# A two-layer decoder on one core: ScalarE takes over the scaled x and fifteen of sixteen final norm steps in the last feed-forward

## The chip, the cores and the metric

One core of a Trainium2 chip runs the whole program. The metric is the device time of one execution in microseconds; lower is better. The engines are TensorE (PE), VectorE (DVE), ScalarE (ACT), GpSimd (POOL) and SyncE (SP, which issues the DMAs). Each has its own instruction queue, works it off in order, and waits for the others by semaphores.

## The reference

Two decoder layers on x of 8 x 256 x 512, each with self-attention, cross-attention and a feed-forward; after each of the six a residual sum and a layer norm, (x - mean) / sqrt(var + 1e-5). The change touches the sixth alone, a feed-forward with 8-bit floats (e4m3) and one scale per tensor:

```python
def _fp8_matmul(x2d, w):
    scale_x = jnp.maximum(jnp.max(jnp.abs(x2d)) / 448.0, 1e-06)
    scale_w = jnp.maximum(jnp.max(jnp.abs(w)) / 448.0, 1e-06)
    x8 = (x2d / scale_x).astype(jnp.float8_e4m3fn)
    w8 = (w / scale_w).astype(jnp.float8_e4m3fn)
    return jnp.matmul(x8.astype(x2d.dtype), w8.astype(x2d.dtype).T) * (scale_x * scale_w)
h = _fp8_matmul(x2d, w_fc)           # 2048 x 512 by 512 x 2048
h = jnp.square(jax.nn.relu(h))
out = _fp8_matmul(h, w_proj)         # 2048 x 2048 by 2048 x 512
x = _layernorm(x + out, axis=-1)     # and this is the output
```

Since h is scaled by its own maximum, no part of the second product can start before all of the first is known.

## The kernel before

The six parts run one after the other; x (2048 rows of 512) stays in SBUF as sixteen tiles of 128 x 512 (`x_all`). The last part, `fp8_ffn_1` (L2096), has two blocks of code with a full stop of all engines between them.

**The first block** (L2135 to L2279) computes the first product into `kept`. x is taken in eight chunks c of two tiles (`x_of(c)`, 128 x 1024). Of each chunk ACT makes `raised` (L2198: the absolute value times a factor, bf16) and POOL makes `value` (L2279: x times the inverse scale, f32); DVE rounds to e4m3 from both, two operations in `round_e4m3` (L1123, L1125); PE turns the result (`turn`, L2159, 8 transposes); ACT copies it out of PSUM into `xT` (L2202). `raised`, `value` and `rounded` have two buffers each, so chunk c waits until chunk c-2 is rounded. Chunks 0 and 1 are done ahead. Then come NB = 4 batches n of 512 columns, each of NG = 8 groups k of 8 matmuls (L2169) into one of three pairs of PSUM banks; ACT evicts each group with Relu (L2215) and DVE takes its maximum (L2247). Within batch n the next two chunks are woven in: DVE rounds them behind k = 1 and 4, PE turns them behind k = 3 and 6, ACT copies them at k = 4 and 6 and makes `raised` of the two after these at k = 5 and 7 (for n = 0 and 1).

**The second block** (L2300 to L2385) handles the 32 groups of `kept` in order, u = 8 n + k. ACT squares a group twice (L2324, L2325), DVE rounds it in two operations (L2347, L2352), and PE multiplies (L2314, 8 matmuls). Rings of RING = 4 buffers join them: ACT may square group u once DVE has rounded group u - 4. A batch's sums lie in PSUM in four tiles t. They are finished while the next batch is rounded: `fin` (DVE: L2331 adds the residual, L164 and L166 take mean and variance), the inverse root on POOL (`root_of`: L174, L176), and `apply` (DVE L181: subtract the mean, multiply by the root, in place). In the batch after, `fin` of tile t stands behind DVE's group k by `FINS`, `apply` by `APPLIES` (L2105). For the last batch all four tiles are finished behind the last group. SP stores each pair of tiles once both are applied (L2382 to L2384).

Of the kernel before, what the change touches and what calls it, by code (L numbers as in the profile page):

```python
# [11 lines left out]
ALU = mybir.AluOpType  # L12
# [7 lines left out]
QT = S // P  # L20
# [2075 lines left out]
def fp8_ffn_1(nc, g, w8, out):  # L2096
# [7 lines left out]
    FINS = {1: 0, 2: 1, 4: 2, 5: 3}  # L2104
    APPLIES = {2: 0, 4: 1, 5: 2, 6: 3}  # L2105

    with ExitStack() as mem:
# [16 lines left out]
        topped, spread = g.sem("f1_top_ready"), g.sem("f1_top_spread")  # L2124
        valued, raised_s = g.sem("f1_x_scaled"), g.sem("f1_x_raised")
        xlinked, xrounded, turned, copied = (g.sem("f1_x_" + n) for n in ("link", "rounded", "turned", "copied"))
# [8 lines left out]
        with nc.Block() as block:  # L2135
# [55 lines left out]
            @block.scalar  # L2191
            def _(eng):
                def raise_x(c):
                    if c == 0:
                        eng.wait_ge(w8.linked, 6)
                    if c >= 2:
                        eng.wait_ge(xrounded, c - 1)
                    eng.activation(raised[c % 2], x_of(c), ACT.Abs, scale=w8.raise_by[:, 0:1]).then_inc(raised_s, 1)  # L2198

                def copy_x(c):  # L2200
                    eng.wait_ge(turned, c + 1)
                    eng.activation(xT[:, :, c * S:(c + 1) * S], g.R[:, 2 + c % 2, :].bitcast(BF16).rearrange("p (k n) -> p k n", k=KD),  # L2202
                                   ACT.Copy).then_inc(copied, 1)

                raise_x(0)
                raise_x(1)
                copy_x(0)
                copy_x(1)
                raise_x(2)
                raise_x(3)  # L2210
                for n in range(NB):
                    for k in range(NG):
                        use = n * NG + k
                        eng.wait_ge(up_full, use + 1)
                        eng.activation(kept[:, n, k, :], pairs[use % 3].rearrange("p j n -> p (j n)"), ACT.Relu).then_inc(up_kept, 1)  # L2215
                        if n < NB - 1 and k in (4, 6):
                            copy_x(2 * n + 2 + (k == 6))
                        if n < NB - 2 and k in (5, 7):
                            raise_x(2 * n + 4 + (k == 7))

            @block.vector
            def _(eng):
                def round_x(c):
                    eng.wait_ge(valued, c + 1)
                    eng.wait_ge(raised_s, c + 1)
                    if c >= 2:
# [44 lines left out]
            @block.gpsimd  # L2271
            def _(eng):
                eng.memset(ones[:, :], 1.0).then_inc(filled, 1)
                for c in range(B):
                    if c == 0:
                        eng.wait_ge(w8.linked, 6)
                    if c >= 2:
                        eng.wait_ge(xrounded, c - 1)
                    eng.tensor_scalar(value[c % 2], x_of(c), w8.inverse[:, 0:1], None, ALU.mult).then_inc(valued, 1)  # L2279

# [6 lines left out]
        downed, summed, stats = g.sem("f1_down_added"), g.sem("f1_sum_ready"), g.sem("f1_stats_link")  # L2287
        applied_v, stored = g.sem("f1_norm_by_vector"), g.sem("out_stored")

# [10 lines left out]
        with nc.Block() as block:  # L2300
# [17 lines left out]
            @block.scalar  # L2318
            def _(eng):
                for u in range(NB * NG):  # L2320
                    group = kept[:, u // NG, u % NG, :]
                    if u >= RING:
                        wait_rounded(eng, u - RING)
                    eng.activation(raised[u % RING], group, ACT.Square, scale=raise_root)  # L2324
                    eng.activation(group, group, ACT.Square, scale=root).then_inc(squared, 1)  # L2325

            @block.vector
            def _(eng):
                def fin(n, t):
# [4 lines left out]
                    if n:  # L2334
                        eng.wait_ge(applied_v, TILES * (n - 1) + t + 1)
                    norm_statistics(eng, stats, TILES * n + t, x_tile(n, t), st[t]).then_inc(gathered, 1)

                def apply(n, t):
                    eng.wait_ge(rooted, before["root"] + TILES * n + t + 1)
                    norm_apply(eng, x_tile(n, t), x_tile(n, t), st[t]).then_inc(applied_v, 1)  # L2340

                links = 0
                for u in range(NB * NG):
# [9 lines left out]
                    if n and k in FINS:  # L2353
                        fin(n - 1, FINS[k])
                    if n and k in APPLIES:
                        apply(n - 1, APPLIES[k])
                for t in range(TILES):
                    fin(NB - 1, t)
                    if t:
                        apply(NB - 1, t - 1)  # L2360
                apply(NB - 1, TILES - 1)

            @block.gpsimd
            def _(eng):
                def root_of(n, t):
                    done = TILES * n + t
                    eng.wait_ge(gathered, before["stats"] + done + 1)  # L2367
                    norm_root(eng, rooting, before["rooting"] + POOL_ROOT_STEPS * done, st[t], 1e-5, g.minus_half[:, :]).then_inc(rooted, 1)
                    eng.wait_ge(rooted, before["root"] + done + 1)

# [9 lines left out]
            def _(eng):  # L2380
                for b in range(B):
                    eng.wait_ge(applied_v, QT * (b + 1))  # L2382
                    dst = out.rearrange("b (t p) d -> p b t d", p=P)[:, b:b + 1]
# [99 lines left out]
```

## Time and profile before

| | |
|---|---|
| median of 3 runs | 2383.47 us (2379.13 to 2386.53) |
| the profiled execution, its own time | 2388.34 us |
| its span, first to last instruction | 2386.4 us |
| first block, from ones L2273 to the last maximum | 2175.1 to 2261.3 us |
| second block, first square to last apply | 2266.8 to 2383.2 us |
| busy share of the whole span: PE, DVE, ACT, POOL | 86%, 68%, 50%, 33% |
| mean granted TensorE clock (share of full speed) | 0.945 |

All times in rows count from the start of the span. The last feed-forward is the last 211 us of it. A row of a timeline gives the start, the duration in us, the engine, the line, what is written <- what is read with their shapes, how many such instructions it merges (x4), and in brackets how long the engine had been idle before and who ended that. Two ACT or DVE instructions in a row overlap a little: the next starts about 0.1 us before the one in front has ended, so steps of the work are read from start to start.

### The profile page before, as it was taken

What the parts mean: (1) busy time and instruction counts of PE and PEld (TensorE: products, weight loads), DVE (VectorE), ACT (ScalarE), POOL (GpSimd) and SP (SyncE); (2) the same over time, 40 slices, a digit from 0 to 9 for tenths busy, and PEclk for the clock granted to TensorE, in tenths of its full rate; (3) what the DMA queues carried; (4) which work ended last, traced back from release to release, by engine and by line L of the source; (5) the groups of instructions that cost most, each with busy time, mean ns of one, the idle gap of its engine ahead of it and who ended that gap; (6) DMA issues with size and microseconds to landing.
All of it is one profiled execution on the core that took longest, in us unless ns stands there. A gap on an engine that the chain in (4) does not pass through costs nothing. (4 is left out here: it accounts for less than half of the span.)

```text
span 2386.4 us, 39689 instructions
## 1 busy us (share of the span) xinstructions
PE 2049.2 (86%) x14893; PEld 1744.1 (73%) x14900; DVE 1627.6 (68%) x3672; ACT 1203.7 (50%) x3119; POOL 780.5 (33%) x817
## 2 busy tenths in 40 slices
PE   6999999379999988799978789999999999984764
PEld 5899988267777777577758678888888988883321
DVE  3677777547767675688865645567676776765798
ACT  3666555256666665334333334445555554343583
POOL 1223222476666664344431111111111112223112
PEclk8999999689999998899989889999999999997998
DMA  4111121200000000521110031224233322100101
GB/s 163 55 54 54 41 72 63 80 5 6 5 5 6 5 1 1 194 98 36 37 37 12 1 141 63 86 93 163 89 111 133 111 80 85 60 21 36 36 18 53
DMA packets 51781, 143.87 MB, mean 60 GB/s; under 512 B 4604, under 2 KB 15869, under 8 KB 46728
## 3 DMA queue, kind: packets, MB, share of 16 engines
q1 hardware_dynamic: 51592, 141.34, 16.6%
q8 instruction: 120, 1.97, 0.3%
q14 instruction: 69, 0.57, 0.1%
HBM read 111.95 MB, written 29.36 MB: 59 GB/s over the span
## 5 line engine op out<-in xcount | busy, mean ns | idle before, releaser
L2032 POOL TENSOR_TENSOR x_probs<-x_probs,x_total 128x512 f32<-128x512 f32 x128 | 133.4, 1042 | 588.3 <-DVE x_total L2002 588.1
L1953 ACT ACTIVATE x_probs<-x_probs,x_nmax 128x256 f32<-128x256 f32 x256 | 128.3, 502 | 259.4 <-DVE x_nmax L1992 259.4
L140 DVE TENSOR_TENSOR x_probsT_lo<-banks,x_probsT_hi 128x512 fp32r<-128x512 f32 x256 | 168.0, 682 | 52.5 <-ACT x_probsT_hi L134 52.1
L134 ACT ACTIVATE x_probsT_hi<-banks 128x512 fp32r<-128x512 f32 x256 | 145.1, 604 | 105.9 <-PE banks L1887 83.3
L597 PE MATMUL banks<-x_turned,x_wq_hi 128*128 128x256 f32 x1024 | 185.8, 283 | 9.8 <-DVE x_turned L140 9.8
L597 PE MATMUL banks<-x_probsT_hi,x_V_hi 128*128 128x256 f32 x512 | 152.0, 297 | 33.5 <-DVE x_probsT_lo L140 33.5
L597 PEld LDWEIGHTS banks<-x_turned,x_wq_hi 128*128 128x128 f32 x1024 | 157.3, 189 | 11.1 <-DVE x_turned L140 11.0
L902 POOL TENSOR_TENSOR x_probs<-x_probs,x_total 128x960 f32<-128x960 f32 (+1 forms) x128 | 131.8, 1051 | 93.8 <-DVE x_total L1054 93.8
L589 POOL TENSOR_TENSOR a_probs<-a_probs,a_total 128x512 f32<-128x512 f32 (+1 forms) x64 | 95.0, 1494 | 174.6 <-DVE a_total L559 174.6
L1011 ACT ACTIVATE x_probs<-banks,x_nmax 128x240 f32<-128x240 f32 x256 | 115.1, 471 | 67.2 <-DVE x_nmax L1042 67.2
L597 PE MATMUL banks<-x_probsT_lo,x_V_hi 128*128 128x256 f32 x512 | 147.5, 288 | 0.0
L597 PE MATMUL banks<-x_probsT_hi,x_V_lo 128*128 128x256 f32 x512 | 147.5, 288 | 0.0
L597 PE MATMUL banks<-x_turned,x_wq_lo 128*128 128x256 f32 x512 | 143.7, 281 | 0.0
L1309 POOL TENSOR_TENSOR f_hid_lo<-f_hid,f_hid_hi 128x256 fp32r<-128x256 f32 x128 | 94.1, 735 | 141.6 <-ACT f_hid_hi L134 141.2
L597 PEld LDWEIGHTS banks<-x_probsT_hi,x_V_hi 128*128 128x128 f32 x512 | 100.5, 196 | 43.1 <-DVE x_probsT_lo L140 41.1
L1290 ACT ACTIVATE f_act<-f_z 128x256 f32<-128x256 f32 x128 | 53.4, 417 | 151.0 <-DVE f_z L1361 150.8
L523 ACT ACTIVATE a_probs<-banks,a_nmax 128x128 f32<-128x128 f32 (+1 forms) x256 | 104.4, 425 | 39.8 <-DVE a_nmax L549 39.3
L1272 PE MATMUL banks<-f_downT,f_hid_hi 128*128 128x512 f32 x256 | 111.0, 434 | 1.6 <-POOL f_hid_lo L1309 1.6
L597 PE MATMUL banks<-x_wo_hi,x_oT_hi 128*128 128x512 f32 x256 | 105.0, 410 | 2.6 <-DVE x_oT_lo L140 2.6
L2314 PE MATMUL banks<-f_weights,f_xT 128*128 128x512 bf16 x256 | 67.2, 413 | 44.2 <-DVE f_xT L2352 44.2
L597 PEld LDWEIGHTS banks<-x_probsT_lo,x_V_hi 128*128 128x128 f32 x512 | 100.7, 197 | 0.9
L597 PE MATMUL banks<-x_wo_lo,x_oT_hi 128*128 128x512 f32 x256 | 101.0, 395 | 0.0
(452 smaller groups left out, 7075.9 us busy)
## 6 DMA issues: line engine op xcount, KB each, us to landing
x_turned<-x_parked SPq DMA_DIRECT2D x24, 1536.0 KB, 6.5
x_parked<-x_turned SPq DMA_DIRECT2D x8, 1536.0 KB, 5.8
x_raw_q<-in_L_xattn_Wq_dram SPq DMA_DIRECT2D x5, 1024.0 KB, 5.2
x_raw_o<-in_L_xattn_Wo_dram SPq DMA_DIRECT2D x5, 1024.0 KB, 8.2
x_all<-in_x_dram SPq DMA_DIRECT2D x2, 2048.0 KB, 18.0
a_sign_raw<-in_L_ffn_W_g_dram SPq DMA_DIRECT2D x8, 512.0 KB, 3.9
f_parked<-a_sign_turned SPq DMA_DIRECT2D x16, 256.0 KB, 2.4
a_sign_raw<-in_L_ffn_W_u_dram SPq DMA_DIRECT2D x8, 512.0 KB, 3.7
```

Source lines behind the costliest of these rows:

```text
L134: return eng.activation(out, in_, ACT.Copy, scale=scale)
L140: return eng.tensor_tensor(out, in_, high.bitcast(F32), ALU.subtract)
L523: ins = eng.activation(probs[u % NP][:, r, 0:keys], banks[:, r, :], ACT.Exp, bias=nmax[:, u, r:r + 1], accum_out=total[:, u, r:r + 1])
L589: eng.tensor_tensor(probs[u % NP][:, :, 0:keys], probs[u % NP][:, :, 0:keys], total[:, u, :].unsqueeze(2).to_broadcast([P, G4, keys]), ALU ...
L597: ins = eng.matmul(out, lhs, rhs, start=start and n == 0, stop=stop and n == len(steps) - 1)
L902: ins = eng.tensor_tensor(tile, tile, total[:, u, n, :].unsqueeze(2).to_broadcast([P, G4, c1 - c0]), ALU.mult)
L1011: eng.activation(probs[u % NP][:, r, 0:MAIN], g.S[:, r, 0:MAIN], ACT.Exp, bias=nmax[:, u, r:r + 1], accum_out=total[:, u, 0, r:r + 1])
L1272: ins = eng.matmul(g.S[:, 2 * b.parity + t, :], h[:, t * P:(t + 1) * P], downT[:, m, :], start=m == 0 and n == 0, stop=m == HT - 1 and n == 1)
L1309: eng.tensor_tensor(hid_lo[buf][:, :], hid[buf][:, :], hid_hi[buf][:, :].bitcast(F32), ALU.subtract).then_inc(low, 1)
L1953: ins = eng.activation(probs[t][r][:, j, :], probs[t][r][:, j, :], ACT.Exp, bias=nmax[:, t, r, j:j + 1], accum_out=total[:, t, r, j:j + 1])
L2032: eng.tensor_tensor(probs[t][r][:, :, :], probs[t][r][:, :, :], total[:, t, r, :].unsqueeze(2).to_broadcast([P, 2, S]), ALU.mult).then_inc ...
L2314: ins = eng.matmul(accumulator(n, t), hidden[u % RING][:, at:at + P], proj[h][:, :, m + j, :], start=k == 0 and j == 0, stop=k == NG - 1 a ...
```

## The change

- `value` of each chunk is made by ACT (`activation` Copy with a scale pointer) just ahead of `raised`, and POOL's L2279 is gone with its semaphore. In the opening, ACT's order is now scale 0, scale 1, copy 0, scale 2, copy 1, scale 3.
- `apply` of fifteen tiles is made by ACT: Identity(x * root + offset), where the offset, -mean * root, is a new 128 x 1 operation on POOL behind L176. In batch n ACT applies tiles 0, 1, 2 of batch n-1 behind its squares k = 5, 6, 7, and tile 3 of batch n-2 behind k = 0. Behind the last square it applies tile 3 of batch 2 and tiles 0 to 2 of batch 3. DVE keeps the last tile's apply.
- `fin` of DVE now waits for ACT's apply of the same tile number one batch back, as `st[t]` is used again; SP's stores wait for ACT's applies, the last one for DVE's too.

```diff
-    APPLIES = {2: 0, 4: 1, 5: 2, 6: 3}
+    APPLIES = {5: 0, 6: 1, 7: 2}
...
-                def raise_x(c):
+                def scale_x(c):
                     if c == 0:
                         eng.wait_ge(w8.linked, 6)
                     if c >= 2:
                         eng.wait_ge(xrounded, c - 1)
-                    eng.activation(raised[c % 2], x_of(c), ACT.Abs, scale=w8.raise_by[:, 0:1]).then_inc(raised_s, 1)
+                    eng.activation(value[c % 2], x_of(c), ACT.Copy, scale=w8.inverse[:, 0:1])
+                    eng.activation(raised[c % 2], x_of(c), ACT.Abs, scale=w8.raise_by[:, 0:1]).then_inc(valued, 1)
...
-                raise_x(0)
-                raise_x(1)
+                scale_x(0)
+                scale_x(1)
                 copy_x(0)
+                scale_x(2)
                 copy_x(1)
-                raise_x(2)
-                raise_x(3)
+                scale_x(3)
...
                         if n < NB - 2 and k in (5, 7):
-                            raise_x(2 * n + 4 + (k == 7))
+                            scale_x(2 * n + 4 + (k == 7))
...
                 eng.memset(ones[:, :], 1.0).then_inc(filled, 1)
-                for c in range(B):
-                    if c == 0:
-                        eng.wait_ge(w8.linked, 6)
-                    if c >= 2:
-                        eng.wait_ge(xrounded, c - 1)
-                    eng.tensor_scalar(value[c % 2], x_of(c), w8.inverse[:, 0:1], None, ALU.mult).then_inc(valued, 1)
...
             @block.scalar
             def _(eng):
+                def apply(n, t):
+                    eng.wait_ge(offset, TILES * n + t + 1)
+                    eng.activation(x_tile(n, t), x_tile(n, t), ACT.Identity, scale=st[t][:, 9:10], bias=st[t][:, 10:11]).then_inc(applied_s, 1)
+
                 for u in range(NB * NG):
...
                     eng.activation(group, group, ACT.Square, scale=root).then_inc(squared, 1)
+                    if n and k in APPLIES:
+                        apply(n - 1, APPLIES[k])
+                    if n > 1 and k == 0:
+                        apply(n - 2, TILES - 1)
+                apply(NB - 2, TILES - 1)
+                for t in range(TILES - 1):
+                    apply(NB - 1, t)
...
                     if n:
-                        eng.wait_ge(applied_v, TILES * (n - 1) + t + 1)
+                        eng.wait_ge(applied_s, TILES * (n - 1) + t + 1)
...
                     if n and k in FINS:
                         fin(n - 1, FINS[k])
-                    if n and k in APPLIES:
-                        apply(n - 1, APPLIES[k])
                 for t in range(TILES):
                     fin(NB - 1, t)
-                    if t:
-                        apply(NB - 1, t - 1)
-                apply(NB - 1, TILES - 1)
+                eng.wait_ge(rooted, before["root"] + TILES * NB)
+                norm_apply(eng, x_tile(NB - 1, TILES - 1), x_tile(NB - 1, TILES - 1), st[TILES - 1]).then_inc(applied_v, 1)
...
-                    eng.wait_ge(rooted, before["root"] + done + 1)
+                    if done < TILES * NB - 1:
+                        eng.wait_ge(rooted, before["root"] + done + 1)
+                        eng.tensor_scalar(st[t][:, 10:11], st[t][:, 6:7], st[t][:, 9:10], -1.0, ALU.mult, ALU.mult).then_inc(offset, 1)
...
                 for b in range(B):
-                    eng.wait_ge(applied_v, QT * (b + 1))
+                    eng.wait_ge(applied_s, min(QT * (b + 1), QT * B - 1))
+                    if b == B - 1:
+                        eng.wait_ge(applied_v, 1)
```

## Rows read from the trace of the kernel before

**Rows 1.** By stretch, busy us (x count) of PE, PEld, DVE, ACT, POOL; clock, DMA share, GB/s

```profile
2190.00:2260.00 70.00, 60.04 (x297) 27.51 (x302) 50.86 (x43) 43.77 (x44) 12.46 (x5) 0.98 0.05 15
2266.00:2374.00 108.00, 67.11 (x256) 24.36 (x256) 99.47 (x114) 68.59 (x64) 23.66 (x24) 0.89 0.08 30
```

**Rows 2.** Timeline of the first block's opening, all engines

```profile
2177.52 2.19 ACT L2198 ACTIVATE f_kept<-x_all,f_raise_by 128x1024 bf16<-128x1024 f32 x2 [15.05 <-DVE f_raise_by L1118]
2177.60 13.48 POOL L2279 TENSOR_SCALAR f_kept<-x_all,f_inverse 128x1024 f32<-128x1024 f32 x4 [2.25 <-DVE f_raise_by L1118]
2180.50 1.23 DVE L1123 SCALAR_TENSOR_TENSOR f_kept<-f_kept 128x1024 f32<-128x1024 bf16 x1 [3.01 <-POOL f_kept L2279]
2181.76 1.94 DVE L1125 SCALAR_TENSOR_TENSOR f_kept<-f_kept 128x1024 bf16<-128x1024 bf16 x1
...
2187.66 1.03 PE L2159 MATMUL banks<-ident,f_kept 128*128 128x128 bf16 x8 [2.87 <-DVE f_kept L1125]
2188.73 1.02 ACT L2202 ACTIVATE f_xT<-banks 128x1024 bf16<-128x1024 bf16 x1 [2.87 <-PE banks L2159]
...
2190.21 8.38 PE L2169 MATMUL banks<-f_xT,f_weights 128*128 128x512 bf16 x31 [1.52 <-ACT f_xT L2202]
```

**Rows 3.** Timelines of ACT, DVE and PE where batch 0 passes into batch 1

```profile
2210.46 1.14 ACT L2198 ACTIVATE f_kept<-x_all,f_raise_by 128x1024 bf16<-128x1024 f32 x1
2211.50 1.01 ACT L2215 ACTIVATE f_kept<-banks 128x1024 f32<-128x1024 f32 x1
...
2212.55 1.22 DVE L2247 TENSOR_REDUCE f_hmax<-f_kept 128x1 f32<-128x1024 f32 x1 [0.73 <-ACT f_kept L2215]
...
2215.18 1.22 DVE L1123 SCALAR_TENSOR_TENSOR f_kept<-f_kept 128x1024 f32<-128x1024 bf16 x1
...
2217.80 0.61 PE L2159 MATMUL banks<-ident,f_kept 128*128 128x128 bf16 x8 [1.40 <-DVE f_kept L1125]
```

**Rows 4.** Groups of ACT by form, whole span: busy us, mean ns | idle before

```profile
L1939 ACT ACTIVATE x_q_value<-x_q_raw,f_inverse 128x512 f32<-128x512 f32 x32 | 23.0, 719 | 0.0
L985 ACT ACTIVATE x_temp<-banks,x_norms_q 128x512 f32<-128x512 f32 x16 | 12.3, 772 | 0.2 <-POOL x_kT_lo L896 0.2
```

**Rows 5.** Timeline of DVE around the first finished tiles of the second block

```profile
2288.41 1.22 DVE L2347 SCALAR_TENSOR_TENSOR f_kept<-f_xT,f_kept 128x1024 f32<-128x1024 bf16 x1
...
2290.88 1.22 DVE L2347 SCALAR_TENSOR_TENSOR f_kept<-f_xT,f_kept 128x1024 f32<-128x1024 bf16 x1
...
2293.34 0.74 DVE L2331 SCALAR_TENSOR_TENSOR x_all<-banks,f_scaled,x_all 128x512 f32<-128x512 f32 x1
...
2294.95 1.19 DVE L2347 SCALAR_TENSOR_TENSOR f_kept<-f_xT,f_kept 128x1024 f32<-128x1024 bf16 x1
...
2299.42 1.22 DVE L2347 SCALAR_TENSOR_TENSOR f_kept<-f_xT,f_kept 128x1024 f32<-128x1024 bf16 x1
```

**Rows 6.** Waits, 2266 to 2374 us: who <- whom: us, times, longest

```profile
DVE f_kept L2347 <- ACT f_kept L2325: 2.7, 1, 2.7
```

**Rows 7.** Timeline of POOL behind the tiles begun at 2293.34 and 2297.39

```profile
2295.12 1.10 POOL L174 TENSOR_SCALAR f_st<-f_st 128x1 f32<-128x1 f32 x1 [67.34 <-DVE f_st L166]
2296.31 1.59 POOL L176 TENSOR_TENSOR f_st<-f_st,minus_half 128x1 f32<-128x1 f32 x1
...
2299.25 0.34 POOL L174 TENSOR_SCALAR f_st<-f_st 128x1 f32<-128x1 f32 x1 [1.35 <-DVE f_st L166]
```

**Rows 8.** Timeline of the tail behind the last group, DVE

```profile
2374.11 0.75 DVE L2331 SCALAR_TENSOR_TENSOR x_all<-banks,f_scaled,x_all 128x512 f32<-128x512 f32 x1 [2.00 <-PE banks L2314]
...
2375.73 0.72 DVE L2331 SCALAR_TENSOR_TENSOR x_all<-banks,f_scaled,x_all 128x512 f32<-128x512 f32 x1
...
2377.74 0.74 DVE L2331 SCALAR_TENSOR_TENSOR x_all<-banks,f_scaled,x_all 128x512 f32<-128x512 f32 x1
...
2382.66 0.55 DVE L181 TENSOR_SCALAR x_all<-x_all,f_st 128x512 f32<-128x512 f32 x1 [0.77 <-POOL f_st L176]
```

**Rows 9.** Timeline of PE in the second block, at the second pair of finished tiles

```profile
2302.03 5.31 PE L2314 MATMUL banks<-f_weights,f_xT 128*128 128x512 bf16 x16 [2.60 <-DVE f_xT L2352]
```

More of the change, by code:

```diff
@@ L2124, in fp8_ffn_1 @@
         topped, spread = g.sem("f1_top_ready"), g.sem("f1_top_spread")
-        valued, raised_s = g.sem("f1_x_scaled"), g.sem("f1_x_raised")
+        valued = g.sem("f1_x_scaled")
         xlinked, xrounded, turned, copied = (g.sem("f1_x_" + n) for n in ("link", "rounded", "turned", "copied"))
@@ L2224, in round_x @@
                     eng.wait_ge(valued, c + 1)
-                    eng.wait_ge(raised_s, c + 1)
                     if c >= 2:
@@ L2287, in fp8_ffn_1 @@
         downed, summed, stats = g.sem("f1_down_added"), g.sem("f1_sum_ready"), g.sem("f1_stats_link")
-        applied_v, stored = g.sem("f1_norm_by_vector"), g.sem("out_stored")
+        offset, applied_s, applied_v = g.sem("f1_norm_offset_ready"), g.sem("f1_norm_by_scalar"), g.sem("f1_norm_by_vector")
+        stored = g.sem("out_stored")
         def wait_rounded(eng, u):
@@ L2319, in _ @@
             def _(eng):
+                def apply(n, t):
+                    eng.wait_ge(offset, TILES * n + t + 1)
+                    eng.activation(x_tile(n, t), x_tile(n, t), ACT.Identity, scale=st[t][:, 9:10], bias=st[t][:, 10:11]).then_inc(applied_s, 1)
                 for u in range(NB * NG):
-                    group = kept[:, u // NG, u % NG, :]
+                    n, k = divmod(u, NG)
+                    group = kept[:, n, k, :]
                     if u >= RING:
@@ L2334, in fin @@
                     if n:
-                        eng.wait_ge(applied_v, TILES * (n - 1) + t + 1)
+                        eng.wait_ge(applied_s, TILES * (n - 1) + t + 1)
                     norm_statistics(eng, stats, TILES * n + t, x_tile(n, t), st[t]).then_inc(gathered, 1)
-                def apply(n, t):
-                    eng.wait_ge(rooted, before["root"] + TILES * n + t + 1)
-                    norm_apply(eng, x_tile(n, t), x_tile(n, t), st[t]).then_inc(applied_v, 1)
                 links = 0
```

## The prediction

> **What bounds the kernel now.** I read the page first. DVE is busy 68% of the whole span and PE 86%, but the change touches only the last 211 us, so the average says little. Next I read the busy time by stretch. While the first product runs (2190 to 2260 us) PE is busy 60.04 of 70 us, DVE 50.86, ACT 43.77, POOL 12.46; while the second is made (2266 to 2374) DVE is busy 99.47 of 108 us and ACT 68.59 [rows 1]. So PE leads the first block and DVE the second, and the timelines must confirm it.
>
> In the second block, DVE waits for ACT once, 2.7 us before its first group, and never again [rows 6]. From start to start a plain group takes 2290.88 - 2288.41 = 2.47 us of DVE, one with a `fin` behind it 2294.95 - 2290.88 = 4.07, one with `fin` and `apply` 2299.42 - 2294.95 = 4.47 [rows 5]. Every DVE operation taken out of this stretch shortens the path, as long as ACT keeps ahead.
>
> In the first block, the opening is a chain: POOL's `value` (until 2180.5), DVE's rounding, PE's turn, ACT's copy, the first matmul at 2190.21 [rows 2]. Later PE runs on without a break except before each of the six turns of chunks 2 to 7: there it waits 1.40 us for DVE's L1125 [rows 3].
>
> **The change part by part.**
>
> *1. The opening.* Before, DVE starts L1123 at 2180.50 behind POOL; L1125 takes 1.94 us beside POOL's next operation, against 1.22 for L1123's kind [rows 2, 3]. ACT's two operations on 128x1024 take 2.19 us together, so 1.04 from start to start and 1.15 the last [rows 2]. I price `value` on ACT like that. Then ACT makes value 0 at 2177.52, raised 0 at 2178.56, done 2179.71; L1123 starts at 2179.75 and L1125 at 2181.0; with POOL gone I give it 1.23, so it ends at 2182.25. The second chunk: ACT is done at 2181.8, DVE starts L1123 at about 2182.15 and ends L1125 at 2184.65. PE's second turn takes 1.03 and ends at 2185.75. Now ACT's order matters: copy 0 can start at 2183.35 (first turn done), takes 0.92 to the next start (1.02 less the overlap of 0.1), then scale 2 takes 2 x 1.04 us, so copy 1 starts at 2186.35, not at 2185.8. Before it started at 2188.73 [rows 2]. **Gain 2.35 us.** If L1125 keeps its 1.94 us without POOL, two of them give back 1.4, but 0.6 of that is hidden behind scale 2: the gain is at least 1.5. Scale 3 ends at 2189.5, ahead of the first eviction, 3.4 us or more behind the first matmul (then at 2187.85).
>
> *2. `value` inside the first block.* Chunks 4 to 7 cost ACT 1.04 us more each, at k = 5 and 7 of batches 0 and 1. At k = 5: the eviction of k = 6 slides by 1.04; PE has three pairs of banks and doesn't need it; the copy behind it slides by about 0.3 and is still done 0.4 before PE's batch ends. Cost nothing; the cover is the third pair of banks. At k = 7: before, ACT starts L2198 at 2210.46 and the next eviction (k = 0 of batch 1) at 2211.50, so the latter comes at 2212.54, 1.04 late; DVE's maximum L2247, before at 2212.55 directly behind it, comes at 2213.6, and with 1.14 us for each of two maxima from start to start, L1123 starts at 2215.9 where it was 2215.18. So rounding is 0.7 us later, and PE, which waited 1.40 us for it at 2217.80, waits 2.10 [rows 3]. This happens for batches 1 and 2. **Cost 2 x 0.7 = 1.4 us**, between 0 (a slack not seen) and the full 4 x 1.04 = 4.2. I take 1.4, since each step has its row.
>
> *3. Twelve applies leave DVE's loop.* Each costs 4.47 - 4.07 = 0.40 to 0.45 us there from start to start [rows 5]; I take 0.43. **Gain 12 x 0.43 = 5.2 us**, if ACT keeps ahead. ACT pays for them: an ACT operation of 128x512 from SBUF with a scale pointer takes 0.72 us, one from PSUM with scale and bias pointers 0.77 [rows 4]; I take 0.75. ACT has 108 - 68.6 us idle here [rows 1], so the amount is no problem; the order may be. An apply at the head of ACT's queue waits for POOL's offset, and the next group's squares are queued behind it, for which DVE waits, and PE behind DVE. The tightest place: `fin` of tile 3 starts on DVE at time F (k = 5). Its L166 is done about 1.7 us later; L174 starts at F + 1.8 and L176 ends at F + 4.56 (2295.12 and 2296.31 + 1.59 against 2293.34) [rows 5, 7]. The offset, a 128x1 operation like L174 but behind a DVE operation of 1.22 us, ends near F + 5.4. ACT, which has squared the group k = 0 long before, applies tile 3 until F + 6.15 and squares group k = 1 until F + 8.35 (2.2 us for the pair). DVE comes to this group at F + 1.61 + 3 x 2.47 = F + 9.0. Margin 0.65 us, at two places (k = 1 of batches 2 and 3); the other applies have more. POOL's chain is covered by the same margins.
>
> *4. The tail.* Four `fin` follow each other on DVE. Without an apply between them the step is 2375.73 - 2374.11 = 1.62 us, with one 2377.74 - 2375.73 = 2.01 [rows 8]; two of the three applies lie between (0.39 each), the third beside POOL's root. **Gain 0.8 us.** The last apply stays on DVE as it is; ACT's apply of tile 2 ends a good 1 us before it (offset 1.62 us ahead of the last tile's root, and 0.75 us on ACT). The last store starts with DVE's apply as before. The store ahead of it starts about 2.6 us before it instead of 3.3; each has 512 KB. Cost nothing, at most a few tenths.
>
> *5. New POOL operations.* Fifteen offsets, off the path except through the DVE. POOL's L174 took 1.10 us while DVE ran L2347, whose end at 2296.14 it survived by 0.08 us: POOL waits for DVE [rows 5, 7]. The other way: the DVE groups with POOL's L174 and L176 beside them are not longer than others (4.07 includes one) [rows 5]. Price 0; from above 12 x 0.35 us = 4.2, if each offset (L174 took 0.34 us when it started ahead of L2347 [rows 7]) holds DVE for its whole length.
>
> The Trainium skill, page "SBUF — State Buffer", section "SBUF: two separate sides", says that DVE and GpSimd share a port pair under an exclusive lock, taken for a whole instruction, and that whoever comes second is blocked entirely. For POOL the trace agrees (1.10 us, ending with L2347). For DVE it would make L1125 at 2181.76 wait for the POOL operation beside it; the row has 1.94 us, a slow-down and not a block. By the rule the sum would be that of rival A.
>
> **The sum.** 2.35 - 1.4 + 5.2 + 0.8 = 6.95, say 7.0 us less. The profiled execution would go from 2388.34 to 2381.3 (span 2386.4 to 2379.4). Against the median shown, 4.9 us lower than the profiled execution, it is 2383.47 - 7.0 = 2376.5 us, 0.29% less. What a measurement of this kernel can tell from no change is about 0.3% (7.2 us), so the forecast sits on that line.
>
> **The rivals.**
>
> *A. POOL's offsets hold DVE.* Twelve in the loop at 0.35 us: 4.2 us back, 2380.7. For: L1125's 1.94 us beside POOL. Against: POOL's 24 small operations in the second block show no such cost. Chance 0.10.
>
> *B. ACT falls behind in the second block.* If POOL gets through only when DVE has no two-operand work, the offset of tile 3 comes only when DVE stops for want of group k = 1 (F + 9.0). Then offset 0.35, apply 0.75, squares 2.2: DVE idle 3.3 us at two places, 6.6 us, 2383.1. For: L176 took 1.59 us. Against: it got through between L2352 and the next L2347. Chance 0.08.
>
> *C. ACT's added work in the first block reaches PE in full.* 4.2 us instead of 1.4, and 2379.3. For: ACT works without a pause from k = 4 to 7. Against: three bank pairs. Chance 0.11.
>
> *D. Slower than before: the clock falls in the first block.* PE waits 2.10 us instead of 1.40 before the turn in batches 1 and 2. In the second block PE is slow behind waits of that length: after 2.60 us, 16 matmuls take 5.31 us, 0.33 each [rows 9], where the first block's PE operations take 60.04 / 297 = 0.20 [rows 1]. A group of 8 is 1.6 us at 0.20 each, and at the lower of the two clock levels (1.2 GHz for 2.4) 1.6 us more. If each of the two longer waits leaves the clock low for the four groups to the batch's end, that is 8 x 1.6 = 12.8 us and 2389.3. It decides from the fifth such group (7.0 us are then gone). Against: PE is busy 60 of 70 us there and was granted 0.98 [rows 1], against 67 of 108 in the second block at 0.89. Chance 0.04.
>
> **How the numbers follow.** Forecast 0.67, A 0.10, B 0.08, C 0.11, D 0.04. The predicted time is the forecast's, 2376.5. Its own spread, from the bounds of the opening (1.5 to 2.35), the loop (0.40 to 0.45 each) and the three runs' scatter (2379 to 2387), is 2372.5 to 2380.5. The range reaches to A and C whole and most of B's side: 2371.5 to 2382. Faster by over 0.3% means below 2376.3: three fifths of the forecast, since what was not priced (matmuls closer together, hence a higher clock) is rather on this side: 0.40, and hardly anything else: 0.41. Slower by over 0.3% needs D or an unknown: 0.05. Within 0.3%: 0.54.
>
> **What would show it.** In the changed trace: the first matmul of L2169 10.35 us behind ACT's first L2198 or its successor, where it was 12.7 (2190.21 - 2177.52); L1125 at 1.23 us in the opening; PE waiting 2.1 us before the first turn of batches 1 and 2 and 1.4 before the others; second block from first square to last apply 110.4 us, where it was 116.45; DVE groups with `fin` at 4.07 and none at 4.47; DVE's L2347 waiting for ACT once only. Wrong it would be if L2347 waits for ACT at k = 1 of batches 2 and 3 (B), if L2347 or L2352 grow beyond 1.23 us (A), if PE waits for L2215 (C), or if matmuls between turns take 0.43 us (D).

## The result, and the profile after

| | before | after |
|---|---|---|
| median of 13 runs each | 2385.43 us (2379.13 to 2390.24) | 2379.01 us (2373.39 to 2384.40) |
| ratio, 95% interval | | 0.997 (0.9961 to 0.9979) |
| the profiled execution, its own time | 2388.34 us | 2379.84 us |
| its span | 2386.4 us | 2377.8 us |

0.3% less is 7.2 us of 2385; the medians themselves differ by 6.4. The predicted gain was 7.0. The predicted time, 2376.5 us, is 2.5 below the measured median and inside the stated 2371.5 to 2382; 2.0 of the 2.5 come from the median of before, which was 2383.47 over 3 runs and is 2385.43 over 13. Each kernel's runs spread over some 10 us, so the medians can't tell the steps apart. All ratios leave out two executions, of 2998 and 3938 us, that came up in the runs for the experiments. The stages of the two profiled executions can tell the steps apart:

| stage, from start to start | before | after | gain | predicted |
|---|---|---|---|---|
| span's start to ACT's first operation of this feed-forward | 2177.52 | 2175.82 | 1.70 | none: nothing is changed there |
| from there to the first weight load for L2169 | 12.28 | 9.88 | 2.40 | 2.35 |
| the weight load to the first turn inside the loop | 10.18 | 10.99 | -0.81 | 0 |
| ACT's first operation to the last maximum, the two rows above included | 82.53 | 82.25 | 0.28 | 0.95 |
| the last maximum to the first square | 6.70 | 6.70 | 0 | 0 |
| the first square to the end of the last apply | 116.46 | 109.82 | 6.64 | 6.0 |

The second and third rows share one point that has to be taken with care. The record of the first matmul of L2169 is missing in the trace of before (its row in [rows 2] has x31, and begins at 2190.21, while the weights were loaded from 2189.80 on), so I count from the weight load. The third row gives back 0.81 of the second row's 2.40: what counts is the fourth row. In these two executions the stages that the change touches gained 0.28 + 6.64 = 6.92 us; the other 1.70 us of the two spans' difference came before the changed code.

The traces of the experiments below show how much of this is the scatter of single executions. Up to the last maximum the first block takes 82.53 and 82.88 us in two traces with POOL's `value`, and 82.25, 82.39 and 82.59 in three with the change's opening and `value` on ACT: a gain of 0.28 is no larger than this spread. The second block takes 116.46, 117.27 and 117.20 us in three traces with DVE's applies, and 109.82 to 110.80 in seven with ACT's. That gain is plain in every pair.

The last maximum and the first square, before and then after (the last applies stand in [rows 8] and with the tail below):

```profile
2260.05 1.22 DVE L2247 TENSOR_REDUCE f_hmax<-f_kept 128x1 f32<-128x1024 f32 x1 [0.51 <-ACT f_kept L2215]
...
2266.75 1.15 ACT L2324 ACTIVATE f_xT<-f_kept,f_raise_by 128x1024 bf16<-128x1024 f32 x1 [6.73 <-PEq L2135]
```

```profile
2258.07 1.22 DVE L2247 TENSOR_REDUCE f_hmax<-f_kept 128x1 f32<-128x1024 f32 x1 [0.51 <-ACT f_kept L2216]
...
2264.77 1.15 ACT L2324 ACTIVATE f_xT<-f_kept,f_raise_by 128x1024 bf16<-128x1024 f32 x1 [6.73 <-PEq L2135]
```

The opening, as [rows 2] before. In this timeline the two products of ACT stand ahead of DVE's rounding:

```profile
2175.82 1.15 ACT L2198 ACTIVATE f_kept<-x_all,f_inverse 128x1024 f32<-128x1024 f32 x1 [15.03 <-DVE f_raise_by L1118]
2176.87 1.13 ACT L2199 ACTIVATE f_kept<-x_all,f_raise_by 128x1024 bf16<-128x1024 f32 x1
...
2178.03 1.22 DVE L1123 SCALAR_TENSOR_TENSOR f_kept<-f_kept 128x1024 f32<-128x1024 bf16 x1 [2.25 <-ACT f_kept L2199]
2179.29 1.23 DVE L1125 SCALAR_TENSOR_TENSOR f_kept<-f_kept 128x1024 bf16<-128x1024 bf16 x1
...
2184.64 1.01 ACT L2203 ACTIVATE f_xT<-banks 128x1024 bf16<-128x1024 bf16 x1
...
2185.70 0.13 PEld L2169 LDWEIGHTS banks<-f_xT,f_weights 128*128 128x128 bf16 x2 [1.97 <-ACT f_xT L2203]
2186.11 0.15 PEld L2169 LDWEIGHTS banks<-f_xT,f_weights 128*128 128x128 bf16 x1 [0.27 <-issue]
...
2190.38 0.15 PEld L2169 LDWEIGHTS banks<-f_xT,f_weights 128*128 128x128 bf16 x1 [0.28 <-issue]
2190.81 4.00 PEld L2169 LDWEIGHTS banks<-f_xT,f_weights 128*128 128x128 bf16 x19 [0.28 <-issue]
```

L1125 takes 1.23 us here, where it took 1.94 beside POOL [rows 2]. The weight loads then stand singly, 0.43 us apart, until 2190.81: eleven such rows. From there nineteen of them take 4.00 us together, 0.21 each. Before, there were seven single rows, until 2193.20. The stretches (columns as in [rows 1]) show what this is:

```profile
2185.70:2191.00 5.30, 5.29 (x13) 1.86 (x14) 0.61 (x1) 3.05 (x3) 0.00 (x0) 0.52 0.00 0
2191.00:2196.00 5.00, 4.30 (x20) 1.76 (x18) 3.64 (x4) 2.71 (x3) 0.00 (x0) 1.00 0.00 0
2188.30:2258.30 70.00, 58.98 (x299) 26.86 (x297) 51.08 (x44) 45.64 (x46) 0.00 (x0) 0.98 0.06 16
2264.00:2366.00 102.00, 68.22 (x255) 24.71 (x256) 93.97 (x102) 76.16 (x76) 38.37 (x36) 0.87 0.08 29
```

The sixth number is the granted clock, as a share of full speed. After the opening's waits PE was granted 0.52, its lower level, for 5.1 us, and then 1.00. Before, by the single rows, the lower level lasted 3.4 us. The last two rows answer to [rows 1]. PE still leads the first block, with POOL out of it. In the second, DVE has 93.97 us of 102 (92.1%; before 99.47 of 108, also 92.1%): it bounds that stretch as before, with twelve operations fewer.

Where batch 0 passes into batch 1, as [rows 3] before:

```profile
2208.21 1.14 ACT L2199 ACTIVATE f_kept<-x_all,f_raise_by 128x1024 bf16<-128x1024 f32 x1
2209.25 1.92 ACT L2216 ACTIVATE f_kept<-banks 128x1024 f32<-128x1024 f32 x2
...
2210.29 2.35 DVE L2247 TENSOR_REDUCE f_hmax<-f_kept 128x1 f32<-128x1024 f32 x2 [1.76 <-ACT f_kept L2216]
2212.55 1.22 DVE L1123 SCALAR_TENSOR_TENSOR f_kept<-f_kept 128x1024 f32<-128x1024 bf16 x1
...
2215.17 0.61 PE L2159 MATMUL banks<-ident,f_kept 128*128 128x128 bf16 x8 [2.05 <-DVE f_kept L1125]
...
2222.36 0.61 PE L2159 MATMUL banks<-ident,f_kept 128*128 128x128 bf16 x8 [1.40 <-DVE f_kept L1125]
```

The eviction starts behind two ACT operations, DVE's two maxima wait for it for 1.76 us (0.73 before), and PE waits 2.05 us before the turn. Before the six turns PE waits 1.39, 1.40, 2.05, 1.40, 2.06 and 1.40 us: two of six have grown by 0.65.

The second block, timelines of POOL, ACT and DVE, answering to [rows 5, 7]:

```profile
2288.89 1.22 DVE L2350 SCALAR_TENSOR_TENSOR f_kept<-f_xT,f_kept 128x1024 f32<-128x1024 bf16 x1
...
2292.96 1.19 DVE L2350 SCALAR_TENSOR_TENSOR f_kept<-f_xT,f_kept 128x1024 f32<-128x1024 bf16 x1
...
2297.01 1.19 DVE L2350 SCALAR_TENSOR_TENSOR f_kept<-f_xT,f_kept 128x1024 f32<-128x1024 bf16 x1
...
2305.95 0.75 DVE L2338 SCALAR_TENSOR_TENSOR x_all<-banks,f_scaled,x_all 128x512 f32<-128x512 f32 x1
...
2310.61 0.74 POOL L2371 TENSOR_SCALAR f_st<-f_st 128x1 f32<-128x1 f32 x1
...
2311.38 0.81 ACT L2317 ACTIVATE x_all<-x_all,f_st 128x512 f32<-128x512 f32 x1 [1.63 <-POOL f_st L2371]
2312.10 1.13 ACT L2324 ACTIVATE f_xT<-f_kept,f_raise_by 128x1024 bf16<-128x1024 f32 x1
2313.14 1.13 ACT L2325 ACTIVATE f_kept<-f_kept,f_scaled 128x1024 f32<-128x1024 f32 x1
...
2314.93 1.22 DVE L2350 SCALAR_TENSOR_TENSOR f_kept<-f_xT,f_kept 128x1024 f32<-128x1024 bf16 x1
```

A group with a `fin` takes 4.07 and 4.05 us of DVE, and none takes 4.47. The lower six lines are the narrowest place, group k = 1 of batch 2: the start of tile 3's `fin`, POOL's offset of this tile, ACT's apply (0.81 us, the next operation 0.72 behind its start), the two squares, ready at 2314.27 (2313.14 + 1.13), and DVE, which wants them at 2314.93: 0.66 us to spare. The waits of this stretch confirm it; DVE waits for ACT once, before its first group, as in [rows 6]:

```profile
DVE f_kept L2350 <- ACT f_kept L2325: 2.7, 1, 2.7
```

The tail, answering to [rows 8]:

```profile
2366.61 0.75 DVE L2338 SCALAR_TENSOR_TENSOR x_all<-banks,f_scaled,x_all 128x512 f32<-128x512 f32 x1 [2.00 <-PE banks L2309]
...
2368.23 0.72 DVE L2338 SCALAR_TENSOR_TENSOR x_all<-banks,f_scaled,x_all 128x512 f32<-128x512 f32 x1
...
2373.13 0.22 POOL L174 TENSOR_SCALAR f_st<-f_st 128x1 f32<-128x1 f32 x1 [0.34 <-DVE f_st L166]
...
2374.04 0.55 DVE L181 TENSOR_SCALAR x_all<-x_all,f_st 128x512 f32<-128x512 f32 x1 [0.99 <-POOL f_st L176]
```

From the first `fin` to the end of the last apply it takes 7.98 us (9.10 before): 1.12 us less. From there to the end of the span it is 3.2 us in both.

### The profile page after: what moved, and what is told of

Same layout as the page of the kernel before. It is cut to its first block and busy times, and to the rows that moved or that the text cites. A ratio compares the mean times of both kernels' runs of the same rounds, so it can differ in the third digit from the quotient of the medians.

```text
span 2377.8 us, 39694 instructions
## 1 busy us (share of the span) xinstructions
PE 2052.3 (86%) x14900; PEld 1744.8 (73%) x14900; DVE 1618.6 (68%) x3657; ACT 1220.5 (51%) x3142; POOL 769.4 (32%) x824
## 3 DMA queue, kind: packets, MB, share of 16 engines
q8 instruction: 120, 1.97, 0.3%
## 5 line engine op out<-in xcount | busy, mean ns | idle before, releaser
L597 PEld LDWEIGHTS banks<-x_probsT_hi,x_V_lo 128*128 128x128 f32 x512 | 101.1, 198 | 0.0
```

Source lines behind the costliest of these rows:

```text
L597: ins = eng.matmul(out, lhs, rhs, start=start and n == 0, stop=stop and n == len(steps) - 1)
```

## The experiments

Kernels run together share the runs of the kernel before, to which each ratio is taken. Its medians were 2387.55 us (35 runs) beside the first four, 2389.87 (17, one of them at 3937.83) beside the next three, and 2384.70 (14) beside the last three.

### One half alone: the applies

The first block as before, with its order of ACT's opening; the second as after. Cut from the edit against after:

```diff
-                    eng.activation(value[c % 2], x_of(c), ACT.Copy, scale=w8.inverse[:, 0:1])
...
+                for c in range(B):
...
+                    eng.tensor_scalar(value[c % 2], x_of(c), w8.inverse[:, 0:1], None, ALU.mult).then_inc(valued, 1)
```

> Second block as in the changed kernel (ACT applies fifteen tiles), first block as before (POOL makes value). My theory: the parts add up and the second block carries most of the gain: first square to last apply 109.8 us as in the changed kernel (116.45 before), the first block as before, so 6.6 us faster than before (ratio 0.9972) and within 1 us of the changed kernel. Rival (the gain comes from the first block, or the two parts need each other): less than 3 us faster than before.

Measured: 2382.70 us (11 runs), ratio 0.9976 (0.9962 to 0.9989). In its trace the second block takes 110.80 us, 5.66 less than before and 0.98 more than after. The 0.98 is one wait: at the tail DVE waited 2.95 us for PE instead of 2.00:

```profile
2369.31 0.75 DVE L2344 SCALAR_TENSOR_TENSOR x_all<-banks,f_scaled,x_all 128x512 f32<-128x512 f32 x1 [2.95 <-PE banks L2315]
```

PE's last 16 matmuls were granted 0.68 (2364.0 to 2369.3 us), where after had 0.98 in the same place (2361.3 to 2366.6). The applies are the larger part of the gain.

### The other half alone: `value` on ACT

The second block as before, the first as after. Cut from the edit against before:

```diff
-                    eng.activation(raised[c % 2], x_of(c), ACT.Abs, scale=w8.raise_by[:, 0:1]).then_inc(raised_s, 1)
+                    eng.activation(value[c % 2], x_of(c), ACT.Copy, scale=w8.inverse[:, 0:1])
+                    eng.activation(raised[c % 2], x_of(c), ACT.Abs, scale=w8.raise_by[:, 0:1]).then_inc(valued, 1)
...
-                    eng.tensor_scalar(value[c % 2], x_of(c), w8.inverse[:, 0:1], None, ALU.mult).then_inc(valued, 1)
```

> First block as in the changed kernel (ACT makes value), second block as before. My theory: the opening wins 2.4 us up to the first matmul, PE gives 0.8 back at a low clock behind it, and the rounding that comes 0.65 us late in batches 1 and 2 takes another 1.3: net 0.3 us faster, not to be told from before; ACT's first activation to the last maximum 82.2 us, where it was 82.5. Rival (the opening's gain is kept and only the chip's scatter hid it): 2.4 us faster or more. Rival (ACT's added work reaches PE in full): 2 us slower.

Measured: 2387.85 us (12 runs), ratio 1.0001 (0.9989 to 1.0012): nothing that could be measured. The trace has the whole pattern of after in the first block (first weight load after 9.90 us; waits before the turns of 1.40, 1.40, 2.06, 1.40, 2.06 and 1.40), and its length up to the last maximum is 82.39 us, against 82.53 before. What the opening gains, the two longer waits and the longer stretch at the low clock give back.

### The opening in the other order

```diff
                 copy_x(0)
-                scale_x(2)
                 copy_x(1)
+                scale_x(2)
```

> The changed kernel, but in the opening ACT copies chunk 1 before it scales chunk 2. My theory: copy 1 stood 0.6 us behind PE's second turn only because of scale 2, so the first weight load comes 9.3 us behind ACT's first activation instead of 9.9; of this PE may lose up to all at the low clock, so 0 to 0.6 us faster than the changed kernel. If the low clock lasts a fixed time from the first matmul on, the 0.6 us stay; if it ends at a time that the start does not move, the first eviction gains 0.6 and the first turn inside the loop nothing. Rival (the scale of chunk 2 is needed early): slower by up to 1 us.

Measured: 2379.47 us (11 runs), ratio 0.997 (0.996 to 0.9981). From the trace, the first weight load and, in batch 2, the matmuls behind the 2.06 us wait:

```profile
2186.89 0.13 PEld L2169 LDWEIGHTS banks<-f_xT,f_weights 128*128 128x128 bf16 x2 [1.38 <-ACT f_xT L2203]
...
2233.79 0.62 PE L2159 MATMUL banks<-ident,f_kept 128*128 128x128 bf16 x8 [2.06 <-DVE f_kept L1125]
2234.23 7.03 PE L2169 MATMUL banks<-f_xT,f_weights 128*128 128x512 bf16 x24
```

The first load comes 9.31 us behind ACT's first operation, 0.57 earlier than in after, so ACT's order was worth what its row in the prediction says. At the first turn inside the loop this kernel was 1.63 us ahead of after (19.24 us behind ACT's first operation instead of 20.87), the rest of it because only six single weight loads came, not eleven. Up to the last maximum the first block still took 82.32 us. The reason stands in the last line: 24 matmuls took 7.03 us, where after needed 5.34, with 0.83 granted from 2233 to 2243 (after: 1.00 in the same place). This is rival D's mechanism, seen at one of the two longer waits of this execution, at 1.7 us instead of the 6.4 that rival D put on each.

### How near the second block is to waiting for ACT

Two useless 128x1 operations on POOL ahead of each offset:

```diff
+                        for i in range(2):
+                            eng.tensor_scalar(st[t][:, 11:12], st[t][:, 6:7], -1.0, None, ALU.mult).then_inc(spare, 1)
+                            eng.wait_ge(spare, 2 * done + i + 1)
                         eng.wait_ge(rooted, before["root"] + done + 1)
                         eng.tensor_scalar(st[t][:, 10:11], st[t][:, 6:7], st[t][:, 9:10], -1.0, ALU.mult, ALU.mult).then_inc(offset, 1)
```

> The changed kernel with two useless 128x1 operations on POOL ahead of each of the fifteen offsets, each waited for. My theory: POOL's small operations cost DVE nothing by themselves, but the offset of tile 3 then comes about 2.5 us later, which uses up the margin of 0.62 us that ACT has at group k = 1 of batches 2 and 3: DVE waits about 1.9 us there, twice, 3.7 us slower than the changed kernel, and DVE's rounding operations stay at 1.19 to 1.23 us. Rival A (POOL's operations hold DVE): 24 more in the loop at 0.26 us or more make DVE's groups longer everywhere, 6 us or more on top. Rival (the margin is much wider than I read it): no change.

Measured: 2382.28 us (12 runs), ratio 0.9981 (0.997 to 0.9993), 2.8 us above the copy-first kernel that ran beside it. DVE has two new waits for ACT in its second block and no third:

```profile
2308.71 0.75 DVE L2338 SCALAR_TENSOR_TENSOR x_all<-banks,f_scaled,x_all 128x512 f32<-128x512 f32 x1
...
2316.61 0.81 ACT L2317 ACTIVATE x_all<-x_all,f_st 128x512 f32<-128x512 f32 x1 [3.49 <-POOL f_st L2374]
...
2319.53 1.23 DVE L2350 SCALAR_TENSOR_TENSOR f_kept<-f_xT,f_kept 128x1024 f32<-128x1024 bf16 x1 [1.76 <-ACT f_kept L2325]
...
2347.43 1.23 DVE L2350 SCALAR_TENSOR_TENSOR f_kept<-f_xT,f_kept 128x1024 f32<-128x1024 bf16 x1 [1.76 <-ACT f_kept L2325]
```

The first two lines are the start of tile 3's `fin` and ACT's apply of this tile. Both waits stand at k = 1 of batches 2 and 3, where the margin was worked out to be narrowest. Counted from the start of tile 3's `fin`, ACT's apply came 7.90 us behind it instead of 5.43, so 2.47 later, and DVE's group k = 1 10.82 instead of 8.98, so 1.84 later: the margin was 0.63 us. So the change does keep free of rival B, by 0.6 us and not by more. The second block took 114.55 us, 4.73 more than after: 3.7 in these two places, as expected, and 1.0 at the tail, which the expectation left out, where DVE's last apply waited 1.97 us for POOL instead of 0.99. The same kernel speaks against rival A: with 15 x 2 more POOL operations, L2350 takes 1210 ns in the mean and L2355 1225, where after has 1208 and 1225. POOL's small operations wait; DVE's don't.

### Half of `value` back on POOL

The last lines are POOL's; the wait ahead of them is DVE's, in `round_x`.

```diff
-                    eng.activation(value[c % 2], x_of(c), ACT.Copy, scale=w8.inverse[:, 0:1])
+                    if c < 4:
+                        eng.activation(value[c % 2], x_of(c), ACT.Copy, scale=w8.inverse[:, 0:1])
...
+                    if c >= 4:
+                        eng.wait_ge(valued_p, c - 3)
...
+                for c in range(4, B):
+                    eng.wait_ge(xrounded, c - 1)
+                    eng.tensor_scalar(value[c % 2], x_of(c), w8.inverse[:, 0:1], None, ALU.mult).then_inc(valued_p, 1)
```

> The changed kernel, but value of chunks 4 to 7 (those woven into the batches) is made by POOL again; chunks 0 to 3 stay on ACT. My theory: the late rounding in batches 1 and 2 comes from ACT's extra 1.04 us at k = 7 alone, so PE's wait before the third and fifth turn in the loop falls from 2.05 to 1.40 us and the kernel is 1.3 us faster than the changed one (too little for the totals, plain in the trace); DVE's rounding stays at 1.22 us beside POOL. Rival (POOL beside DVE slows the rounding, as at 1.94 us in the opening before): L1125 at 1.9 us and no gain.

Measured: 2379.65 us (12 runs), ratio 0.9967 (0.9953 to 0.9981). Its profiled execution came at a mean granted clock of 0.642 and took 2998 us, so its trace says nothing of this question, and the kernel was run again:

> The kernel of e5 once more, since its profiled execution came out at a mean clock of 0.642 and says nothing of 1.3 us. The expectation is that of e5: PE's wait before the third and fifth turn in the loop 1.40 us instead of 2.05, DVE's L1123 and L1125 at 1.21 to 1.23 us beside POOL's value. Rival: L1125 at 1.9 us and no gain.

Measured: 2376.97 us (9 runs), ratio 0.997 (0.9958 to 0.9982). In the trace the turn of batch 1 is back at the old wait:

```profile
2217.25 0.61 PE L2159 MATMUL banks<-ident,f_kept 128*128 128x128 bf16 x8 [1.40 <-DVE f_kept L1125]
```

So are all six. From ACT's first operation to the last maximum it takes 80.93 us, after 82.25: 1.32 less, where the two waits had grown by 1.31 together. Both traces have eleven single weight loads in the opening, so the clock there does not blur this comparison. That settles whose cost the 2.05 us are: ACT's extra operation at k = 7. POOL's operation starts only when L1125 has ended (it waits for it), so the pair never runs side by side here, and whether POOL would slow L1125 in the loop as in the opening stays open.

### The waits that were there all along

The change makes two of PE's six waits longer, but all six, 8.4 us, stood before it. They are DVE's order: a chunk is rounded behind the maximum of k = 1, and PE turns it behind k = 3. Rounding one group earlier, in the kernel after (all lengths of the first block here run to the last maximum):

```diff
-                    if n < NB - 1 and k in (1, 4):
-                        round_x(2 * n + 2 + (k == 4))
+                    if n < NB - 1 and k in (0, 3):
+                        round_x(2 * n + 2 + (k == 3))
```

> The changed kernel, but DVE rounds the two chunks of a batch behind k = 0 and 3 instead of 1 and 4; PE's turns stay behind k = 3 and 6. My theory: PE waits for DVE's rounding before each of the six turns only because it stands one group too late, so these waits (four of 1.40 us, two of 2.05) go: to 0 in batch 0 and for the second chunks, to about 0.7 for the first chunks of batches 1 and 2. But ACT then has no pause before copy 2n+3, whose end PE awaits at the start of the next batch: 1.1 us new waiting twice. Net 6.1 us faster than the changed kernel. Rival (DVE is nearly full in the first block, so the waits only move to the next turn or to the last maximum): less than 2 us faster.

Measured: 2371.00 us (6 runs), ratio 0.9948 (0.9929 to 0.9967). The first block takes 76.02 us, 6.23 less than after. Four turns come without a wait, two with 0.56 us; two new waits of 1.22 and 1.07 us appear at the start of batches 1 and 2, for the copy at k = 6 of the batch in front, which stands behind ACT's pair at k = 5.

With ACT's pairs put where they hold nobody, and the copy-first opening:

```diff
-                        if n < NB - 2 and k in (5, 7):
-                            scale_x(2 * n + 4 + (k == 7))
+                        if n < NB - 2 and k == 3:
+                            scale_x(2 * n + 4)
+                        if 0 < n < NB - 1 and k == 0:
+                            scale_x(2 * n + 3)
```

> The changed kernel with three edits: DVE rounds behind k = 0 and 3; ACT scales the first chunk of the next batch behind k = 3 and the second chunk of this batch behind k = 0 (instead of k = 5 and 7 of the batch before); in the opening it copies chunk 1 before it scales chunk 2. My theory: no wait of PE is left before the six turns nor between the batches: 4 x 1.40 + 2 x 2.05 = 9.7 us, and 0.6 in the opening, so about 10 us faster than the changed kernel and 0.7% faster than the one before. With PE's waits gone the low clock seen once behind a wait of 2.06 us has no place either. Rival (ACT, with 13.5 us of work per batch of 14.7, comes late with a copy or an eviction): PE waits for L2216 or L2203 and half of it is lost.

Measured: 2371.78 us (6 runs), ratio 0.9937 (0.9918 to 0.9956). By the trace there is no wait before any turn and none for a copy, and the first block takes 70.68 us, 11.57 less than after. Run again with fresh runs of before:

> The kernel of e7 once more, for its total: its six times came at mean clocks of 0.943 (five) and 0.951 (one), while those of before spread over 0.941 to 0.950. My theory: the trace's 11.9 us against the changed kernel (19 us against before) are in the total too, ratio to before 0.992; rival (the scatter hides a loss elsewhere, for instance more PE work per time lowers the clock in the parts before it): ratio 0.994 or more again, and lower clocks than before.

Measured: 2365.86 us (6 runs), ratio 0.9914 (0.9898 to 0.993), first block 70.68 us. This version beats both kernels.

The same edit of DVE's order on the kernel before, with nothing of the change:

> The kernel before the change with one edit: DVE rounds the two chunks of a batch behind k = 0 and 3 instead of 1 and 4. value stays on POOL, apply on DVE. My theory: the six waits of 1.40 us before PE's turns go and nothing comes in their place, as ACT has only raised to make at k = 5 and 7: 8.4 us faster than before (ratio 0.9965), more than the whole change gave. Rival (ACT's lack of time before copy 2n+3 is there without value too): 1 us of new waits at the start of batches 1 and 2, 6 us faster.

Measured: 2375.16 us (6 runs), ratio 0.9962 (0.9948 to 0.9977). PE's timeline around the first turn of batch 1:

```profile
2200.47 7.08 PE L2169 MATMUL banks<-f_xT,f_weights 128*128 128x512 bf16 x31 [0.18 <-ACT f_xT L2202]
2207.39 0.61 PE L2159 MATMUL banks<-ident,f_kept 128*128 128x128 bf16 x8
2207.84 5.34 PE L2169 MATMUL banks<-f_xT,f_weights 128*128 128x512 bf16 x24
```

The turn has no wait; two new ones of 0.18 us stand for all that ACT's order costs here. The first block takes 75.08 us, 7.45 less than before, although its stretch of single weight loads was the longer (13 against 7). So an edit of two lines in one queue, which leaves every engine's work as it is, gave about as much as the whole change: by the ratios 9.1 us (0.0038 of 2384.7) against 7.2, with intervals that overlap.

## Why the prediction was right, step by step

- **What bounds.** Right in both blocks. DVE lost twelve applies and stays at 92.1% of the second block's loop; DVE waits for ACT there once.
- **1, the opening (2.35).** The gain to the first weight load was 2.40 us, and L1125 took the 1.23 that it was given. The sign given for it, the first matmul 10.35 us behind ACT's first operation, read [rows 2] wrongly: the matmul at 2190.21 is not before's first, whose record is missing, and after has its first at 9.89 us. What the step left out is that PE comes out of the opening at its lower clock. From the first load on, that lasted 3.4 us before and 5.1 after; by the second eviction (L2215 at 2195.17 before, L2216 at 2191.88 after, less the 1.70 of scatter) only 1.6 us of the 2.40 were left. Whether the change causes this 0.8 us is not shown: with the old opening 7, 9 and 13 single weight loads were seen in three kernels, with the new one 11, 12, 13, 11 and 11, with copy-first 6, 8 and 8, so that the same code alone varies by six loads. What governs the stretch's length stays open.
- **2, `value` in the loop (cost 1.4).** 1.31 measured, at the two places named, 2.05 and 2.06 us against 2.10 forecast; at k = 5 nothing, as said. Half of `value` back on POOL takes the cost away, so its cause is shown.
- **3, twelve applies (5.2).** From the first square to DVE's last rounding it takes 98.62 us instead of 104.14: 5.52, or 0.46 each instead of 0.43. The margin at the narrowest place was forecast at 0.65 us; the rows give 0.66 and the delay experiment, which breaks exactly there, 0.63.
- **4, the tail (0.8).** 1.12 measured. Two steps of 2.01 and 2.03 us became 1.58 each (0.43 and 0.45 instead of 0.39). The other 0.24 lies behind the last `fin`, where POOL's L174 takes 0.22 us instead of the 0.35 it took with DVE's apply beside it; the step had put that stretch at nothing.
- **5, POOL's offsets (0).** Right: DVE's rounding operations have not grown (1208 and 1225 ns in the mean, before 1217 and 1225). An offset takes 0.26 us when DVE is at a `fin` and 0.74 beside a rounding operation: it is POOL that waits.
- **The sum.** Forecast 6.95 us; 0.28 + 6.64 = 6.92 in the two traces. The two misses, 0.7 us short in the first block and 0.6 over in the second, cancel, so the agreement to 0.03 us is luck. The same stage of the same code varies between executions by 0.3 us in the first block and by 1.0 in the second; the mechanism is confirmed stage by stage, the second decimal is not.

Of the rivals, A is refuted by the lengths of L2350 and L2355, B by the single wait for ACT, C by the wait of 2.05 us at two turns only. D was seen once and small, at one of the eight waits of 2.05 or 2.06 us in four traces.

The Trainium skill, page "SBUF — State Buffer", section "SBUF: two separate sides", puts a DVE operation with two inputs in SBUF and a GpSimd operation that reads SBUF under an exclusive lock: whichever starts first holds it for its whole length, and the other is blocked. For POOL this case agrees: the offset at 2310.61 took 0.74 us and ended 0.13 behind DVE's L2350. For DVE no run shows such a block. The small POOL operations show nothing against the rule either, since each of the waits read here has POOL as the second; of POOL at work when DVE starts, only L1125 at 2181.76 [rows 2] tells, and it was slowed to 1.94 us, not blocked.

The change's first part, `value` on ACT, turned out to be worth nothing measurable alone (ratio 1.0001). The forecast had it at 2.35 - 1.4 = 0.95 us, and yet I read the row of PE's 1.40 us wait [rows 3] only for how the change would lengthen it, not for what it was worth by itself.

## What to carry to other kernels

Price a moved operation by the start-to-start step of its queue, then walk what stands behind it until the first consumer, and write down the margin: here it was right to a few hundredths of a microsecond, and a delay of two small operations was enough to use it up. Where the engine that bounds a stretch waits at all, find the order that makes it wait before moving work between engines: six waits of 1.4 us were worth about as much as all the moved operations together. And where runs scatter by 10 us over changes of 5, compare stages of the traces, from a start to a start, and set apart what comes before the changed code.

## What the runs showed of the hardware

- TensorE's clock behind the opening's waits stays at its lower level for a stretch that varies between executions of the same code (7, 9 and 13 weight loads of 0.43 us with the opening of before). Each kernel's runs spread over some 10 us, and in the runs of before the mean granted clock goes from 0.941 (about 2390 us) to 0.951 (2381).
- In the second block the lower level falls on different groups from one execution to the next. PE's last 16 matmuls were granted 0.98 in the execution of after and 0.68 in that of the kernel with the applies alone, which made the block 1.0 us longer.
- A `tensor_scalar` of 128x1 on POOL took 0.22 to 0.27 us with DVE at a `fin` and up to 1.11 beside DVE's rounding operations, which kept their 1.19 to 1.23 us.
- In batch 2, a wait of 2.06 us of PE left the clock at 1.00 in the execution of after, and at 0.83 over the next 10 us in that of the copy-first kernel. Of the eight waits of this length in four traces this was the only one followed by a low clock; none of the waits of 1.40 us was.
- One execution of the kernel with half of `value` on POOL had a mean granted clock of 0.642 and took 2998 us instead of 2380. One of before took 3937.83 us at a mean granted clock of 0.923, which a clock so near the usual one does not explain. What caused either stays open.
